# A graph layer on one core: the last edge column of every tenth tile, fetched by SyncE row by row

## The chip, the core and the metric

The kernel runs on one core of a Trainium2 chip. The metric is the device time of one execution in microseconds (us), the median of several runs. A core has five engines with an instruction list each: TensorE (PE in the profile, its weight loads PEld), VectorE (DVE), ScalarE (ACT), GpSimd (POOL) and SyncE (SP). They meet through semaphores. Data moves by DMA: an engine issues a transfer, the transfer runs on the core's 16 DMA engines, and its end raises a semaphore by 16.

## The reference: what is computed

One layer of an attention network over a graph with 12500 nodes of 64 features and 400000 edges. Every edge goes from a node src to a node dst and has 64 features of its own; the edges are sorted by dst.

```python
h_src = nfeats[src]
h_dst = nfeats[dst]
z_att = concatenate([h_src, h_dst, efeats], axis=-1)
e = leaky_relu(z_att @ W_attn + b_attn, negative_slope=0.01)[:, 0]
m = concatenate([h_src, efeats], axis=-1) @ W_ne
emax = segment_max(e, dst, num_segments=N)
ex = exp(e - emax[dst])
denom = segment_sum(ex, dst, num_segments=N)
alpha = ex / denom[dst]
z = segment_sum(alpha[:, None] * m, dst, num_segments=N)
out = relu(concatenate([nfeats, z], axis=-1) @ W_out)
# and then: layernorm(x + out)
```

For each edge one row of x is needed, that of its source node. That is the gather `nfeats[src]`.

## The kernel before

**Tiles.** The edges are cut into 391 tiles of 1024 edges (the last has 640). A tile lies on 128 partitions with J = 8 edges each, so it has eight columns. A ring V of ten slots (RING) holds for each tile the gathered source rows (Vx, eight columns of 64 numbers and a one) and the edge's own features (Ve). Ten tiles are a turn; there are 39 turns and one last tile.

**GpSimd** (L370 to L394) fills Vx: for each tile it waits for the tile's source indices (idx_in) and for a free slot (v_free), and then issues eight indirect transfers at L372, each of which brings 128 rows of x to the 128 partitions. In the loop that starts at L381 these are 80 a turn. Their ends raise h_in of the slot.

**SyncE** (L248 to L353) issues all other loads. Its list for the step of a tile t (function `step`, L306) is: wait until VectorE has the edge scores of tile t - 7 (u_done), store them to memory (L265); load the dst numbers of that tile to all partitions (L260); wait for the store and spread the scores to all partitions (L270); load the source indices of tile t + 3 (L254); wait until slot t is free (v_free) and load the edge features of tile t (L257). SyncE takes its list strictly in order, so a wait holds up all that follows.

**VectorE**, for each tile n (`supertile`, L684): L658 weighs the edges of the window before, L697 to L712 find the bounds of the new window from the spread scores (L705 waits for u_in), L663 to L674 add the sums of earlier windows. Then it makes the scores of tile n + 2: it waits for that tile's edge features and gathered rows (L722 to L725), multiplies them by the attention weights (L594), sums (L599) and raises u_done.

**ScalarE** makes the exponentials and copies of turned weights, **TensorE** turns the weights (L837) and multiplies them with the rows in V (L844), and tells when a slot is free. At the head of a turn VectorE, ScalarE and TensorE each load a list of counts from SBUF into registers (`counts`).

Of the kernel before, what the change touches and what calls it, by code (L numbers as in the profile page):

```python
# [27 lines left out]
P = 128  # L28
# [17 lines left out]
KEEP = 1e30  # L46
TINY = 1e-30
CB = 14


def graph_attention(nc, x, src, dst, ef, w_ne, w_att, b_att, w_out, out):
# [10 lines left out]
    NR = NB - 8 * OCT  # L62
    assert TURNS * RING == NT - 1 and JL * P + (NT - 1) * ST == E and 4 < JL < J
    assert 0 < NR <= 4 and OCT >= 4 and OCT % 2 == 0 and E >= ST
    assert YT * YS == PAIRS and 2 * PAIRS == NB and YS <= RING and YT < TURNS - 1
    chunks = [(b, min(CB, NB - b)) for b in range(0, NB, CB)]

    ctx = ExitStack()
    with ctx:
        def sb(name, shape, dt=F32):  # L70
            return ctx.enter_context(nc.sbuf_tensor(name, shape, dt))
# [36 lines left out]
        Vx = Vs[:, :, 0:J * XW].rearrange("p s (j w) -> p s j w", w=XW)  # L108
        Ve = Vs[:, :, EF_AT:EF_AT + J * F].rearrange("p s (j f) -> p s j f", f=F)
        srcs = sb("srcs", [P, RING, J], U32)  # L110
        dbc = sb("dbc", [P, 2, ST], I32)
        ubc = sb("ubc", [P, 2, ST])
        dnone = sb("dnone", [P, ST - JL * P], I32)
# [53 lines left out]
        idx_in = [sem(f"idx_in{s}") for s in range(RING)]  # L167
        ef_in = [sem(f"ef_in{s}") for s in range(RING)]
        h_in = [sem(f"h_in{s}") for s in range(RING)]
        bounds_out = sem("bounds_out")  # L170
        trip_in = sem("trip_in")
        lowf_in = sem("lowf_in")
# [56 lines left out]
        def freed(s, k):  # L229

            return k + (1 if s == RING - 1 else 0)

        def width(o):

            return 8 if not isinstance(o, int) or 0 <= o < OCT else NR if o == OCT else 0
# [12 lines left out]
        @block.sync  # L248
        def _(sp):

            full = NT - 1

            def load_src(t, s):
                sp.dma_start(srcs[:, s, :], edge_rows(src, t).rearrange("(p j) -> p j", j=J).bitcast(U32)).then_inc(idx_in[s], 16)  # L254

            def load_ef(t, s):
                sp.dma_start(Ve[:, s, :, :], (ef[bass.ds(t * ST, ST), :]).rearrange("(p j) f -> p j f", j=J)).then_inc(ef_in[s], 16)  # L257

            def load_dst(t, r):
                sp.dma_start(dbc[:, r, :], edge_rows(dst, t).rearrange("(a e) -> a e", a=1).broadcast_to((P, ST))).then_inc(d_in[r], 16)  # L260

            def store_scores(n, r):

                sp.wait_ge(u_done, n + 1)
                sp.dma_start(scores[r, :].rearrange("(p j) -> p j", j=J), u[:, r, :]).then_inc(u_out, 16)  # L265

            def spread_scores(n, r):

                sp.wait_ge(u_out, 16 * n + 16)
                sp.dma_start(ubc[:, r, :], scores[r:r + 1, :].broadcast_to((P, ST))).then_inc(u_in[r], 16)  # L270

            for s in range(2):
                load_src(s, s)
            sp.dma_start(wa[:, :], w_att.rearrange("a b -> b a").broadcast_to((P, 3 * F))).then_inc(w_in, 16)
            sp.dma_start(ba[:, :], b_att.rearrange("(a b) -> a b", a=1).broadcast_to((P, 1))).then_inc(w_in, 16)
            sp.dma_start(wne[:, :], w_ne[:, :]).then_inc(w_in, 16)
            sp.dma_start(wo_z[:, :], w_out[F:2 * F, :]).then_inc(w_in, 16)
            for s in range(2, RING):
                load_src(s, s)
            sp.wait_ge(wo_cleared, 1)  # L280
            for i in range(2):
                sp.dma_start(wo_xx[i * F:(i + 1) * F, i * F:(i + 1) * F], w_out[0:F, :]).then_inc(w_in, 16)

            for s in range(3):
                load_ef(s, s)
            for r in range(2):
                load_dst(r, r)

            sp.wait_ge(bounds_ready, 2)
            sp.dma_start(bounds_i.rearrange("(c p) k -> p c k", p=P), bi[:, :, :]).then_inc(bounds_out, 16)  # L290
            sp.dma_start(bounds_f.rearrange("(c p) k -> p c k", p=P), bf[:, :, :]).then_inc(bounds_out, 16)
            for s in range(3, 6):
                load_ef(s, s)
            sp.wait_ge(bounds_out, 32)
            sp.dma_start(trip[:, :], bounds_i.rearrange("t k -> (t k)").rearrange("(a b) -> a b", a=1)).then_inc(trip_in, 16)
            sp.dma_start(lowf[:, :, :], bounds_f[0:NT, :].rearrange("t k -> (t k)").rearrange("(a b) -> a b", a=1).broadcast_to((P, NT * 2)).rearrange("p (t k) -> p t k", k=2)).then_inc(lowf_in, 16)
            for n in range(2):
                store_scores(n, n)
                spread_scores(n, n)
            for s in range(6, RING):  # L300
                load_ef(s, s)
            for n in range(2, LEAD):
                store_scores(n, n % 2)
                load_dst(n, n % 2)
                spread_scores(n, n % 2)
            def step(k, s):  # L306

                t, n, r = RING * k + s, RING * k + (s - RING + LEAD), (s + LEAD) % 2
                store_scores(n, r)
                load_dst(n, r)  # L310
                spread_scores(n, r)
                if not isinstance(k, int) or s + AHEAD < RING:
                    ahead = (s + AHEAD) % RING
                    sp.wait_ge(h_in[ahead], 16 * J * (k + (1 if s + AHEAD >= RING else 0)))
                    load_src(t + AHEAD, ahead)
                sp.wait_ge(v_free[s], freed(s, k))
                load_ef(t, s)

            for s in range(AHEAD):
                sp.wait_ge(h_in[s], 16 * J)  # L320
                load_src(RING + s, s)
            with sp.Fori(1, TURNS - 1) as k:
                for s in range(RING):
                    step(k, s)
            for s in range(RING):
                if s == RING - AHEAD:
                    sp.wait_ge(h_in[0], 16 * J * TURNS)
                    sp.dma_start(srcs[:, 0, 0:JL], src[full * ST:E].rearrange("(p j) -> p j", j=JL).bitcast(U32)).then_inc(idx_in[0], 16)
                step(TURNS - 1, s)

            for s in range(RING - LEAD):
                n = full - RING + LEAD + s
                store_scores(n, n % 2)
                load_dst(n, n % 2)
                spread_scores(n, n % 2)
                if s == 0:
                    sp.wait_ge(v_free[0], TURNS)
                    sp.dma_start(Ve[:, 0, 0:JL, :], ef[full * ST:E, :].rearrange("(p j) f -> p j f", j=JL)).then_inc(ef_in[0], 16)
            sp.wait_ge(u_done, full + 1)
            sp.dma_start(scores[full % 2, 0:JL * P].rearrange("(p j) -> p j", j=JL), u[:, full % 2, 0:JL]).then_inc(u_out, 16)  # L340
            sp.wait_ge(dnone_set, 1)
            sp.dma_start(dbc[:, full % 2, 0:JL * P], dst[full * ST:E].rearrange("(a e) -> a e", a=1).broadcast_to((P, JL * P))).then_inc(d_in[full % 2], 16)
            sp.dma_start(dbc[:, full % 2, JL * P:ST], dnone[:, :]).then_inc(d_in[full % 2], 16)
            spread_scores(full, full % 2)

            for o in range(OCT):
                sp.wait_ge(rows_ready, o + 1)
                sp.dma_start(out[o * 8 * P:(o + 1) * 8 * P, :].rearrange("(b p) f -> p b f", p=P), y0[:, 8 * o:8 * o + 8, :]).then_inc(out_done, 16)
            sp.wait_ge(rows_ready, OCT + 1)
            n = NR - 1  # L350
            outs = OCT + 1
            if n:
                sp.dma_start(out[8 * OCT * P:(NB - 1) * P, :].rearrange("(b p) f -> p b f", p=P), y0[:, 8 * OCT:NB - 1, :]).then_inc(out_done, 16)  # L353
                outs += 1
            sp.dma_start(out[(NB - 1) * P:N, :], y0[0:NL, NB - 1, :]).then_inc(out_done, 16)
            sp.wait_ge(out_done, 16 * outs)

        @block.gpsimd
        def _(pool):
# [14 lines left out]

            for s in range(RING):
                pool.wait_ge(idx_in[s], 16)
                gather(s, J)
            if TURNS > 1:
                arrived = pool.alloc_register("arrived")
                behind = pool.alloc_register("behind")  # L380
                with pool.Fori(1, TURNS) as k:  # L381
# [4 lines left out]
                    for s in range(RING):  # L386
                        pool.wait_ge(pool_step, 2)
                        pool.wait_ge(idx_in[s], indices)

                        pool.wait_ge(v_free[s], k if s < RING - 1 else passed)  # L390
                        gather(s, J)
            pool.wait_ge(idx_in[0], 16 * TURNS + 16)
            pool.wait_ge(v_free[0], TURNS)
            gather(0, JL)  # L394
# [138 lines left out]
        def _(dve):  # L533
# [150 lines left out]
            def supertile(k, s, left, y_steps=None):  # L684
# [35 lines left out]
                if left >= 2:  # L720
                    done = t + 3 if isinstance(t, int) else produced
                    dve.wait_ge(ef_in[s2], 16 * k2 + 16)  # L722
                    if not isinstance(t, int):
                        dve.reg_mov(produced, t + 3)
                    dve.wait_ge(h_in[s2], 16 * J * k2 + 16 * (J if left != 2 else JL))  # L725
                    if y_steps is not None:
                        dve.wait_ge(y_ready, y_steps + 1)
                    edge_product(s2).then_inc(prod_done, 1)
# [210 lines left out]
```

## Time and profile before

| | |
|---|---|
| time, median of 3 runs | 4009.97 us (4007.27 to 4010.44) |
| the profiled execution: time | 4021.12 us |
| its span in the trace | 4019.2 us |
| busy in the span: GpSimd, VectorE | 2972.2 us (74%), 2837.8 us (71%) |
| busy in the span: TensorE, ScalarE | 2260.2 us (56%), 2020.9 us (50%) |
| indirect transfers issued by GpSimd | 3125 |
| mean granted TensorE clock | 0.592 |

The profile comes from one execution; its span runs from the first to the last instruction and is 2 us shorter than the execution's own time. Transfers that an engine only issues are not counted as its busy time: SyncE has no busy time at all there, and its work is seen in the timeline (rows with SPq) and in its waits. GpSimd's gathers are counted.

### The profile page before, as it was taken

How to read it: one execution, taken by the hardware profiler on the slowest of the kernel's cores; microseconds unless marked ns; L12 is line 12 of the kernel's file. 1: busy time of each engine (PE TensorE's matmuls, PEld its weight loads, DVE VectorE, ACT ScalarE, POOL GpSimd, SP SyncE). 2: the span in 40 equal slices, each digit the busy share in tenths (PEclk: the TensorE clock that was granted, in tenths of full speed). 3: DMA queues.
4: the chain of work that ended last, by engine and by line, in shares of the span. 5: the costliest groups of instructions: out<-in, count | busy, mean ns of one | idle time of the engine just before them, and what ended most of it. 6: DMA issues, size and time to landing. Idle time of an engine off the chain costs nothing.

```text
span 4019.2 us, 47762 instructions
## 1 busy us (share of the span) xinstructions
PE 2260.2 (56%) x9822; PEld 2005.2 (50%) x9823; DVE 2837.8 (71%) x5649; ACT 2020.9 (50%) x3433; POOL 2972.2 (74%) x3133
## 2 busy tenths in 40 slices
PE   2666655555555555555555555555555555555556
PEld 1555555544454444454444444544444544454456
DVE  8776666666766767676676766676767676766777
ACT  2665555544454444444444444444444444444446
POOL 7777777777777777777777777777777777777770
PEclk9665556556556565555655555555655556555557
DMA  6655555555555555555555555555555555555542
GB/s 166 177 173 156 159 157 156 160 158 157 158 157 157 157 157 157 157 157 157 158 157 157 157 157 157 157 158 157 157 157 157 157 157 158 157 157 157 158 147 66
DMA packets 409354, 627.14 MB, mean 156 GB/s; under 512 B 208412, under 2 KB 208796, under 8 KB 409332
## 3 DMA queue, kind: packets, MB, share of 16 engines
q1 hardware_dynamic: 296260, 519.51, 40.7%
q0 software_dynamic: 100000, 102.60, 12.3%
q10 hardware_dynamic: 13072, 4.80, 0.6%
q14 instruction: 16, 0.13, 0.0%
q8 instruction: 6, 0.10, 0.0%
HBM read 621.58 MB, written 4.81 MB: 156 GB/s over the span
## 4 chain that ended last, share of the span: by engine, by line
POOL 73%; issue 24%; DVE 1%; PE 1%; POOLq 1%; ACT 0%; DMA 0%; DVEq 0%
POOL V L372 73%; POOLq L390 0%; PE psE L909 0%; POOLq L381 0%; PE psT L902 0%; PE psG L844 0%; DVE y L801 0%; DVE var L782 0%; DMA V<-in_x_dram,srcs 0%; DVE y L778 0%; DVE mean L791 0%; DVE y L798 0%; DVE prod L785 0%; DMA srcs<-in_src_dram 0%; ACT zb L522 0%
## 5 line engine op out<-in xcount | busy, mean ns | idle before, releaser
L372 POOL DMA_INDIRECT V<-in_x_dram,srcs x3125 | 2971.2, 951 | 956.0 <-issue 952.9
L844 PE MATMUL psG<-V,pT 128*128 128x130 f32 x6250 | 1461.4, 427 | 366.6 <-DVE psS L663 366.6
L844 PEld LDWEIGHTS psG<-V,pT 128*128 128x128 f32 x6250 | 1361.5, 330 | 506.1 <-DVE psS L663 506.1
L837 PE MATMUL psT<-ident,e 128*128 128x128 f32 x3125 | 720.8, 404 | 1286.3 <-DVE e L658 1286.3
L448 ACT COPY pT<-psT 128x512 f32<-128x512 f32 x784 | 420.9, 589 | 1714.8 <-PE psT L837 1708.9
L837 PEld LDWEIGHTS psT<-ident,e 128*128 128x128 f32 x3125 | 573.8, 215 | 1392.7 <-DVE e L658 1392.7
L594 DVE TENSOR_TENSOR prod<-V,psM 128x512 f32<-128x512 f32 x782 | 502.4, 684 | 637.6 <-DMA V<-in_x_dram,srcs 621.8
L658 DVE TENSOR_TENSOR e<-zb,psE 128x1024 f32<-128x1024 f32 x392 | 478.8, 1221 | 259.4 <-DVE u L599 162.1
L705 DVE CUSTOM_DVE_ANT_0 um<-ubc,psS 128x1024 f32<-128x1024 f32 x391 | 477.6, 1221 | 20.2 <-ACT psS L461 19.3
L599 DVE TENSOR_REDUCE u<-prod 128x8 f32<-128x1024 f32 x391 | 477.0, 1220 | 13.5
L469 ACT ACTIVATE psE<-um,ebias 128x1024 f32<-128x1024 f32 x391 | 437.2, 1118 | 12.8
L461 ACT ACTIVATE psS<-dbc,nbias 128x1024 f32<-128x1024 int32 x391 | 437.1, 1118 | 12.7
L470 ACT ACTIVATE zb<-um,ebias 128x1024 f32<-128x1024 f32 x391 | 443.2, 1133 | 0.0
L669 DVE TENSOR_TENSOR acc<-acc,psS 128x260 f32 x393 | 167.4, 426 | 59.0 <-DVE psS L663 21.9
L674 DVE TENSOR_TENSOR acc<-acc,alpha 128x260 f32 x392 | 168.9, 431 | 56.2
L663 DVE TENSOR_TENSOR psS<-psG,half 128x260 f32<-128x260 f32 x393 | 171.4, 436 | 3.0 <-PE psT L888 1.8
L712 DVE SCALAR_TENSOR_TENSOR node<-keep,nn,node (+1 forms) x391 | 87.8, 225 | 69.0 <-DVE nn L710 67.4
L459 ACT ACTIVATE nbias<-nidbias,wshift 128x1 f32 x391 | 110.6, 283 | 46.5 <-issue 45.9
L467 ACT ACTIVATE ebias<-wnode,nn 128x3 f32<-128x3 f32 x391 | 120.5, 308 | 6.4 <-DVE nn L710 6.1
L473 ACT ACTIVATE alpha<-half,ebias 128x2 f32 x391 | 109.7, 281 | 0.0
L708 DVE SCALAR_TENSOR_TENSOR bounds<-slopes,cmax,wnode 128x3 f32<-128x3 f32 x391 | 87.5, 224 | 14.0
L700 DVE TENSOR_TENSOR wnode<-picked 128x3 f32<-128x3 f32 x391 | 64.7, 165 | 13.6
(97 smaller groups left out, 524.7 us busy)
## 6 DMA issues: line engine op xcount, KB each, us to landing
ubc<-scores SPq DMA_DIRECT2D x391, 512.0 KB
dbc<-in_dst_dram SPq DMA_DIRECT2D x390, 512.0 KB, 4.0
V<-in_edge_attr_dram SPq DMA_DIRECT2D x390, 256.0 KB, 2.8
V<-in_x_dram,srcs POOLq DMA_INDIRECT x3125
srcs<-in_src_dram SPq DMA_DIRECT2D x390, 4.0 KB
scores<-u SPq DMA_DIRECT2D x390, 4.0 KB
out_dram<-y SPq DMA_DIRECT2D x12, 256.0 KB
xt<-in_x_dram ACTq DMA_DIRECT2D x6, 448.0 KB, 14.2
```

The costliest lines, as they stand in the source:

```text
L372: nc.gpsimd.indirect_dma_start(Vx[:, s, j, 1:XW], None, x[:, :], bass.IndirectOffsetOnAxis(ap=srcs[:, s, j:j + 1], axis=0)).then_inc(h_in[ ...
L448: nc.scalar.copy(pT[:, i, :], psT[:, i, :]).then_inc(pt[i], 1)
L461: nc.scalar.activation(psS[:, :], dbc[:, s % 2, :], ACT.Square, bias=nbias[:, 0:1], scale=FAR).then_inc(sq_done, 1)
L469: nc.scalar.activation(psE[:, :], um[:, :], ACT.Exp, bias=ebias[:, 1:2], scale=SLOPE)
L470: nc.scalar.activation(zb[:, :], um[:, :], ACT.Exp, bias=ebias[:, 0:1]).then_inc(e_done, 1)
L594: last = nc.vector.tensor_tensor(prod[:, k * J * F:(k + 1) * J * F].rearrange("p (j f) -> p j f", f=F), rows, wa_v[:, k:k + 1, :].broadcas ...
L599: return nc.vector.tensor_reduce(u[:, i, :], prod[:, :].rearrange("p (k j f) -> p j k f", k=2, f=F), AXY, ALU.add)
L658: nc.vector.tensor_tensor(e1[:, :], zb[:, :], psE[:, :], ALU.max).then_inc(mx_done, 1)
L663: nc.vector.tensor_tensor(shares, psG[:, 0:AW].unsqueeze(1).broadcast_to((P, 2, AW)), half[:, bass.ds(tb, 1), :].rearrange("p a k -> p (a ...
L705: nc.vector.tensor_tensor_reduce(out=um[:, :], in0=ubc[:, r, :], in1=psS[:, :], scale=1.0, scalar=-3e38, op0=ALU.subtract, op1=ALU.max, ac ...
L837: last = nc.tensor.transpose(psT[:, i, (j - 4 * i) * P:(j - 4 * i + 1) * P], e1[:, 0:n * P].rearrange("q (p j) -> q j p", j=n)[:, j, :], i ...
L844: last = nc.tensor.matmul(psG[:, 0:AW], pT[:, i, (j - 4 * i) * P:(j - 4 * i + 1) * P], V[:, LEADIN + s * SLOT + XW * j:LEADIN + s * SLOT + ...
```

## The change

Slot 9 of the ring (OWN) is gathered differently. GpSimd issues only seven of its eight columns (`gathers`), so it issues 79 gathers a turn. The eighth column's 128 rows are fetched by SyncE. It first loads the 128 source indices of that column into one partition (`rowi`). In `load_rows` it loads 19 of them into registers, and issues for each a transfer of one row of x, with the register as offset, to one partition of Vx. The 128 rows are spread over seven steps of SyncE's loop: 19 rows in the step of slot 9 itself, behind its load of edge features, then 19 in each of the steps of slots 0 to 4 and 14 in that of slot 5, each between the load of source indices and the wait for the free slot. VectorE waits for the four semaphores of these rows before the edge product of such a tile.

```diff
+OWN = RING - 1
+BUNCH = 19
+BUNCHES = -(-P // BUNCH)
...
+        rowi = sb("rowi", [1, P], I32)
...
+        rowi_in = sem("rowi_in")
+        row_in = [sem(f"row_in{q}") for q in range(4)]
...
+        def gathers(s):
+
+            return J - 1 if s == OWN else J
...
+            row = [sp.alloc_register(f"row{i}") for i in range(BUNCH)]
+
+            def load_row_indices(t):
+
+                sp.dma_start(rowi[:, :], edge_rows(src, t).rearrange("(p j) -> j p", j=J)[J - 1:J, :], allow_slow_non_contiguous=True).then_inc(rowi_in, 16)
+
+            def load_rows(k, c):
+
+                first, last = c * BUNCH, min(P, (c + 1) * BUNCH)
+                sp.load(row[0:last - first], rowi[0:1, first:last])
+                for i in range(last - first):
+                    p = first + i
+                    at = sp.snap(row[i], min_val=0, max_val=N - 1)
+                    sp.dma_start(Vx[p:p + 1, OWN, J - 1, 1:XW], x[bass.ds(at, 1), :]).then_inc(row_in[p // 32], 16)
...
+            load_row_indices(OWN)
...
-                    sp.wait_ge(h_in[ahead], 16 * J * (k + (1 if s + AHEAD >= RING else 0)))
+                    sp.wait_ge(h_in[ahead], 16 * gathers(ahead) * (k + (1 if s + AHEAD >= RING else 0)))
                     load_src(t + AHEAD, ahead)
+                if s < BUNCHES - 1:
+                    load_rows(k - 1, s + 1)
                 sp.wait_ge(v_free[s], freed(s, k))
+                if s == OWN:
+                    sp.wait_ge(rowi_in, 16 * k + 16)
                 load_ef(t, s)
-
+                if s == OWN - 1:
+                    load_row_indices(t + 1)
+                if s == OWN:
+                    load_rows(k, 0)
+
+            sp.wait_ge(rowi_in, 16)
+            load_rows(0, 0)
...
-                gather(s, J)
+                gather(s, gathers(s))
...
-                        gather(s, J)
+                        gather(s, gathers(s))
...
-                    dve.wait_ge(h_in[s2], 16 * J * k2 + 16 * (J if left != 2 else JL))
+                    dve.wait_ge(h_in[s2], 16 * gathers(s2) * k2 + 16 * (gathers(s2) if left != 2 else JL))
+                    if s2 == OWN:
+                        for q in range(4):
+                            dve.wait_ge(row_in[q], 512 * k2 + 512)
```

How this stands in the built programs, first on SyncE, in the loop, the step of slot 0 before. A row is line, operation, tile written and read, with the semaphore it waits for; ISA here is a fused register instruction.

```order
L265 DMA scores<-u 128x8 [waits u_done]
L260 ISA
L260 DMA dbc<-in_dst_dram 128x1024
L269 ISA
L270 DMA ubc<-scores 128x1024 [waits u_out]
L314 REGISTER_ALU
L254 ISA [waits h_in3]
L254 DMA srcs<-in_src_dram 128x8
L257 ISA [waits v_free0]
L257 DMA V<-in_edge_attr_dram 128x512
```

The same step of the changed kernel, up to its second row. The last two rows of it come 19 times in the step before the wait for v_free0.

```order
L276 DMA scores<-u 128x8 [waits u_done]
L271 ISA
L271 DMA dbc<-in_dst_dram 128x1024
L280 ISA
L281 DMA ubc<-scores 128x1024 [waits u_out]
L341 REGISTER_ALU
L265 ISA [waits h_in3]
L265 DMA srcs<-in_src_dram 128x8
L292 TENSOR_LOAD rowi
L295 ISA
L296 DMA V<-in_x_dram 1x64
```

Between the load of source indices and the edge features there is now a register load and 19 pairs of a register instruction and a row transfer; nothing that stood in the step has changed its place against its neighbours.

On VectorE, in the changed kernel, the edge product of a tile in slot 9 (prod is the product, u the scores):

```order
L763 ISA [waits ef_in9]
L767 ISA [waits h_in9]
L633 TENSOR_TENSOR prod<-V,psM 128x512 [waits row_in2,row_in3,row_in1,row_in0]
L633 TENSOR_TENSOR prod<-V,psM 128x512
L638 TENSOR_REDUCE u<-prod 128x8 [waits prod_done]
```

The first product now waits for the rows; the scores behind it, for which SyncE waits at the head of a step, wait with it.

## Rows read from the trace of the kernel before

**Rows 1.** The page: DMA in all; the chain that ended last, by engine.

```profile
DMA packets 409354, 627.14 MB, mean 156 GB/s; under 512 B 208412, under 2 KB 208796, under 8 KB 409332
...
POOL 73%; issue 24%; DVE 1%; PE 1%; POOLq 1%; ACT 0%; DMA 0%; DVEq 0%
```

**Rows 2.** The page's groups: line, engine, operation | busy us, mean ns | idle before, releaser.

```profile
L372 POOL DMA_INDIRECT V<-in_x_dram,srcs x3125 | 2971.2, 951 | 956.0 <-issue 952.9
```

**Rows 3.** Timeline of VectorE, first tile of a turn: start us, us, line, operation.

```profile
2041.91 1.22 DVE L658 TENSOR_TENSOR e<-zb,psE 128x1024 f32<-128x1024 f32 x1 [2.42 <-issue]
...
2047.25 1.28 DVE L594 TENSOR_TENSOR prod<-V,psM 128x512 f32<-128x512 f32 x2 [0.27 <-issue]
2048.57 1.22 DVE L599 TENSOR_REDUCE u<-prod 128x8 f32<-128x1024 f32 x1
2050.24 1.22 DVE L658 TENSOR_TENSOR e<-zb,psE 128x1024 f32<-128x1024 f32 x1 [0.45 <-DVE u L599]
```

**Rows 4.** Waits: engine, line <- waited for: us in total, times, longest.

```profile
DVE prod L594 <- DMA V<-in_x_dram,srcs: 621.8, 333, 3.1
...
DVE e L658 <- DVE u L599: 162.1, 351, 0.5
...
DVE e L658 <- issue: 94.9, 39, 3.2
...
ACT nbias L459 <- issue: 45.9, 32, 2.1
```

**Rows 5.** Waits of SyncE's issues.

```profile
SPq L265 <- DVE u L599: 1620.5, 390, 17.8
SPq L257 <- PEq L869: 1077.0, 376, 5.0
SPq L270 <- DMA scores<-u: 235.8, 384, 2.8
```

**Rows 6.** Timeline of SyncE, one step and the next step's start.

```profile
2010.34 0.33 SPq L265 DMA_DIRECT2D scores<-u  x1
2010.86 0.33 SPq L260 DMA_DIRECT2D dbc<-in_dst_dram  x1
2011.76 0.33 SPq L270 DMA_DIRECT2D ubc<-scores  x1
2012.29 0.33 SPq L254 DMA_DIRECT2D srcs<-in_src_dram  x1
2015.59 0.33 SPq L257 DMA_DIRECT2D V<-in_edge_attr_dram  x1
2019.33 0.33 SPq L265 DMA_DIRECT2D scores<-u  x1
```

**Rows 7.** Timeline of SyncE at the start: eight index transfers; trip and the next.

```profile
3.85 6.04 SPq L254 DMA_DIRECT2D srcs<-in_src_dram  x8
...
31.75 0.30 SPq L295 DMA_DIRECT2D trip<-bounds_i  x1
32.09 0.34 SPq L296 DMA_DIRECT2D lowf<-bounds_f  x1
```

**Rows 8.** The page's DMA issues: count, KB each, us to landing.

```profile
V<-in_edge_attr_dram SPq DMA_DIRECT2D x390, 256.0 KB, 2.8
```

More of the change, by code:

```diff
@@ L64, in graph_attention @@
     assert 0 < NR <= 4 and OCT >= 4 and OCT % 2 == 0 and E >= ST
+    assert BUNCHES <= RING - LEAD
     assert YT * YS == PAIRS and 2 * PAIRS == NB and YS <= RING and YT < TURNS - 1
@@ L338, in _ @@
                     sp.dma_start(Ve[:, 0, 0:JL, :], ef[full * ST:E, :].rearrange("(p j) f -> p j f", j=JL)).then_inc(ef_in[0], 16)
+                if s < BUNCHES - 1:
+                    load_rows(TURNS - 1, s + 1)
             sp.wait_ge(u_done, full + 1)
```

## The prediction

> **What bounds the kernel now.** I read the chain of waits first: 73% of it is one line, GpSimd's gather, and 24% is issue time in front of it [rows 1]. The group of that line has 3125 gathers with 2971.2 us busy and 956.0 us of idle time before them, which the engine spent issuing [rows 2]. So one gather costs (2971.2 + 956.0) / 3125 = 1.257 us, and GpSimd waits for nobody. A turn of the ring is ten tiles of eight gathers: 80 x 1.257 = 100.5 us. With 391 tiles that is the span, less the start and the last part.
>
> Next I asked who stands right behind. VectorE waits 621.8 us in 333 waits for gathered rows before its edge product [rows 4], so it keeps up. Its own time for one tile is read where it did not wait: from the L658 that starts at 2041.91 to the next at 2050.24 is 8.33 us [rows 3]. At the head of each turn it loads twenty counts into registers; the idle time there is 94.9 us over 39 turns, 2.43 us each, against 162.1 / 351 = 0.46 us on the other tiles [rows 4]. The load of twenty costs 1.97 us.
>
> Then SyncE, which the page does not count as an engine and which the change loads. Its waits are 1620.5 us for the scores (u_done), 1077.0 us for a free ring slot and 235.8 us for the scores' way to memory [rows 5]. The first two are its room: 2697.5 / 390 = 6.9 us a step, 69 us a turn. Its work in a step is in the timeline [rows 6]: scores at 2010.34, dst at 2010.86, the spread at 2011.76 (behind the scores' round trip), src at 2012.29, and the edge attributes at 2015.59, when the slot came free.
>
> **What goes.** Slot 9 is gathered with seven columns, not eight. It is filled by 39 tiles (9, 19, ... 389), so GpSimd loses 39 x 1.257 = 49 us, and its turn becomes 79 x 1.257 = 99.3 us. That is all that can be won.
>
> **What comes, on SyncE.** Per turn there are 128 one-row transfers, each behind one fused register instruction, seven loads of 19 (the last 14) indices into registers, and one transfer of 128 indices. No row of before shows a one-row transfer with a register offset on SyncE, so it is bounded.
> - Below: the transfer onto one partition, trip, is 0.30 us, and the next starts 0.34 us after it [rows 7]. With the register instruction free, 0.34 us a row.
> - Above: eight index transfers back to back took 6.04 us at the start, 0.76 us each [rows 7].
> - Nearest: in the loop src follows the spread with one register instruction and an offset in a register, as a row will: 2012.29 - 2011.76 = 0.53 us, 0.33 of it the transfer, so 0.2 for the rest [rows 6]. With trip's 0.30 in place of 0.33 that is 0.50 us. I take 0.50.
>
> The loads of 19 registers are near VectorE's 1.97 us for twenty; ScalarE's loads of ten leave 45.9 / 32 = 1.43 us of idle time [rows 4]. Both gaps hold the jump back to the loop's head as well; ten registers more cost 1.97 - 1.43 = 0.54 us, so by the slope alone 19 would be 1.03 us. I take 1.9 us and keep 1.03 and 1.97 as ends.
>
> The Trainium skill gives `tensor_load` a floor of about 600 ns ("DMA: Bandwidth & Descriptors", Latency and other measured facts). Both gaps in this trace are more than twice that; with the floor as the price the turn worked out below would be, as an estimate, 7 x 1.3 = 9 us shorter and the time 355 us less.
>
> Alone, 128 x 0.50 + 7 x 1.9 = 77 us a turn against 69 us of room. But the room is not where the rows are: seven of the ten steps carry them all, and SyncE takes its list in order. Behind the rows in a step stand the edge attributes, and behind these the next tile's scores and their spread, without which VectorE can't go on with that tile. So a step that is longer than a gathered tile (10.05 us) delays VectorE, and the light steps can't give it back, since their scores exist only after VectorE has done another tile. The turn, from SyncE's own list:
> - Steps 0 to 4, full: 1.95 from the scores to src [rows 6], 0.52 for src, 1.9 load, 19 x 0.50 = 9.5, and 0.52 for the edge attributes, whose slot is long free by then: 14.4 us, five times 72.0.
> - Step 5, the last 14 rows: 1.95 + 0.52 + 1.9 + 7.0 = 11.4 us. These rows are the last of the tile whose edge product comes next on VectorE. So this product waits for them: 1.4 us to land (what scores takes from its issue to the spread, 2010.34 to 2011.76 [rows 6]), then product and sum, 2.5 us (prod at 2047.25 to 2049.79 [rows 3]), until the next scores exist: 15.3 us.
> - Steps 6 to 8, light, at VectorE's pace: 3 x 8.33 + 1.97 for its counts = 27.0 us.
> - Step 9: its rows stand behind the edge attributes, which leave 5.25 us after the scores (2010.34 to 2015.59 [rows 6]): 5.25 + 0.52 + 1.9 + 9.5 = 17.2 us.
>
> The sum is 131.5 us a turn. GpSimd's 99.3 us vanish under it. Against 100.5 us that is 31.0 us more, 39 times: 1209 us. The profiled execution took 4021 us, so it becomes 5230; the median of the runs is 11 us lower, 5219. I forecast 5220 us.
>
> **What the rest costs.** The 128 indices of a turn are fetched a step ahead in a light step: nothing, and if that cover fails, one round trip of about 1.4 us a turn, 55 us in all. VectorE's four new waits stand before the edge product; queued behind them are the score sum, its u_done and the next tile, on which ScalarE and TensorE hang. That is the wait already in step 5. The src and edge loads run some seven tiles ahead; they come later but not late. The 4992 rows carry 1.3 MB beside 627 MB [rows 1]. What I leave out is that in full steps the edge attributes (2.8 us to landing [rows 8]) leave just before the next scores; the longest wait for a scores' round trip is 2.8 us [rows 5] against a mean of 0.6, so a full step may grow by up to 2.2 us, 11 us a turn. That is in the upper end.
>
> Each 0.01 us of the row is 1.28 us a turn and 50 us of the time. With 0.34 a row and loads of 1.03 us: 52.4 + 12.2 + 27.0 + 13.3 = 104.9 us a turn, 4180 us. With 0.62 a row, or 0.53 and the longer round trips: about 147 us, some 5820 us.
>
> **The rivals.**
> 1. Faster: SyncE's room swallows the rows. The turn above is 67.5 + 128 times the row's cost, so GpSimd still sets the pace if a row costs under (99.3 - 67.5) / 128 = 0.25 us, or under 0.30 us with loads of 1.03 us. Then it is 4010 - 49 = 3961 us. For it: trip was not followed by a stall, and a row is narrower than any transfer shown. Against: no transfer of SyncE in this trace takes under 0.30 us. Chance 0.08; and 0.02 that it ends within 0.2% of before.
> 2. The waits overlap better than I say, and only SyncE's sum counts. Its work without the rows is 1.95 + 0.53 + 0.52 = 3.0 us a step, 30 us a turn; with 77 us, 107 us, 39 x 6.5 = 254 us more: about 4265. For it: the scores are stored two tiles ahead. Against: two tiles of lead are 17 us, and the full steps overrun by 7 x 4. Chance 0.10.
> 3. The register load costs its slope alone, 1.03 us, and the rest of the gaps that I read belongs to the jump at the loop's head, which SyncE's bunches don't make: 7 x 0.87 = 6 us less, a turn of 125.4 us, 971 us more, 4980. For it: both gaps shown stand at a loop's head. Against: ScalarE's load of ten would then be under half of its gap. Chance 0.10. The Trainium skill's floor, above, leans the same way.
> 4. The rows back up in SyncE's transfer queue, as the eight index transfers did: 0.76 us a row, 33 us more a turn than forecast, 6500 us. Against: those stood behind wide transfers at the start. Chance 0.08.
>
> **How the numbers follow.** The forecast keeps 0.62, its own range 4700 to 5750 (0.40 to 0.60 us a row). The range of 8 in 10 runs from the lower bound of the turn to the longer round trips: 4180 to 5820; left out are rival 1 with its even case, 0.10, rival 4, 0.08, and a little of the tail. Within 0.2%, 8 us, no change can be told from none. Faster 0.08, same 0.02, slower 0.90.
>
> **What would show it.** Right: GpSimd's gathers wait for free slots, and the chain of waits runs through SyncE; row transfers start 0.47 to 0.55 us apart; a gap of about 1.9 us stands before each bunch; steps of 14 us, seven in ten; VectorE waits for spread scores in full steps, and for the rows once a turn. Wrong: rows 0.30 us apart or closer, or an untouched GpSimd chain at 99.3 us a turn. If the rows are 0.50 us apart and the turn is still near 107 us, the overlap was misjudged and not the price.

## The result, and the profile after

The changed kernel takes 5603.19 us (5600.80 to 5606.78), the kernel before 4008.70 us: 1.3975 times the time, with a 95% interval of 1.3957 to 1.3993. The forecast was 5220 us, with 4180 to 5820 as range. So it is slower by the mechanism that was forecast, and with a loss a third larger than forecast (1594 us for 1210).

The page of the changed kernel: the instruction transfers, the chain that ended last by engine and by line, and the group of the gathers.

```profile
q14 instruction: 240, 1.97, 0.1%
...
SPq 47%; issue 19%; DVE 17%; DMA 12%; DVEq 3%; PE 1%; ACT 1%; ACTq 1%; PEld 0%; PEldq 0%
SPq L296 22%; SPq L292 16%; DMA scores<-u 10%; SPq L295 4%; DVE prod L633 4%; DVE u L638 3%; DVE um L744 3%; SPq L268 2%; SPq L265 2%; SPq L281 1%; DVE psS L702 1%; DVEq L777 1%; DVE acc L708 1%; DMA V<-in_x_dram 1%; DVE e L697 1%
...
L411 POOL DMA_INDIRECT V<-in_x_dram,srcs x3086 | 2927.2, 949 | 2509.8 <-PEq L911 1653.6
```

The chain has left GpSimd [rows 1] and runs through SyncE's own list. The gathers still take 0.95 us each, but in front of them stand 2509.8 us of idle time where there were 956.0 [rows 2], and most of it now waits for TensorE to free a slot. GpSimd's 39 gathers fewer are worth nothing.

SyncE's waits, in the same form as [rows 5]:

```profile
SPq L276 <- DVE u L638: 428.4, 160, 17.3
SPq L281 <- DMA scores<-u: 404.0, 389, 3.6
SPq L268 <- PEq L911: 383.1, 114, 5.0
```

The wait for the scores fell from 1620.5 to 428.4 us and that for a slot from 1077.0 to 383.1 (a further 103.1 us of it stand at another line, for slot 9): SyncE is now late where it was early. Only the wait for the scores' round trip grew, from 235.8 to 404.0 us. Who waits for SyncE is seen in the waits of the others:

```profile
POOL V L411 <- PEq L911: 1653.6, 288, 19.8
...
DVE um L744 <- DMA ubc<-scores: 1044.3, 140, 9.2
...
DVE prod L633 <- DMA V<-in_x_dram: 738.4, 39, 20.9
```

GpSimd waits for free slots, VectorE for the spread scores, and once a turn (39 times) for the last rows, 738.4 / 39 = 18.9 us each. In 69 further waits, 411.1 us, VectorE's line L744 waits for ScalarE, which waits in its turn for the dst numbers (2049.9 us) that SyncE loads just behind the scores. The timeline of SyncE shows why: the step of slot 9 from its edge features on, the whole step of slot 0, the spread in that of slot 1, and the row part of slot 3's (start us, us, line, operation).

```profile
2750.98 0.33 SPq L268 DMA_DIRECT2D V<-in_edge_attr_dram  x1
2753.34 8.20 SPq L296 DMA_DIRECT2D V<-in_x_dram  x19
2764.23 0.37 SPq L276 DMA_DIRECT2D scores<-u  x1
...
2766.04 0.33 SPq L281 DMA_DIRECT2D ubc<-scores  x1
2766.66 0.33 SPq L265 DMA_DIRECT2D srcs<-in_src_dram  x1
2771.30 7.86 SPq L296 DMA_DIRECT2D V<-in_x_dram  x19
2779.36 0.36 SPq L268 DMA_DIRECT2D V<-in_edge_attr_dram  x1
2779.84 0.36 SPq L276 DMA_DIRECT2D scores<-u  x1
...
2782.03 0.33 SPq L281 DMA_DIRECT2D ubc<-scores  x1
...
2815.51 0.33 SPq L265 DMA_DIRECT2D srcs<-in_src_dram  x1
2817.91 8.09 SPq L296 DMA_DIRECT2D V<-in_x_dram  x19
```

The step of slot 0 takes 2779.84 - 2764.23 = 15.6 us, where a gathered tile takes 10.05. Its 19 rows take 2779.36 - 2771.30 = 8.06 us, 0.42 us each. Between src and the first row lie 4.64 us in this step, but 2.40 us in that of slot 3. The chain of waits has the register loads (L292) as pieces of their own:

```profile
2706.29 3.06 SPq L292
...
2715.06 1.17 DMA V<-in_x_dram
...
2761.72 2.41 issue
...
2767.03 4.09 SPq L292
...
2815.90 1.80 SPq L292
```

A load of the same 19 registers takes 4.09 us in one step and 1.80 us in another; the load of 14 takes 3.06. The last row lands 1.17 us after its issue. And at the loop's jump there are 2.41 us of issue time in which SyncE does nothing. Last, the row transfer itself (line, operation, count: shortest, median and longest in ns); a register move of 29 ns stands at the same line before each:

```profile
L296 SPq DMA_DIRECT2D V<-in_x_dram x4992: 224/228/308, 73.0 to 5508.5; - x200
```

### The profile page after: what moved, and what is told of

The parts are those of the page before. It is cut to its first block, busy times and chain, and to the rows that moved or that the text cites. A ratio compares the mean times of both kernels' runs of the same rounds, so it can differ in the third digit from the quotient of the medians.

```text
span 5599.3 us, 63276 instructions
## 1 busy us (share of the span) xinstructions
PE 2165.4 (39%) x9822; PEld 1936.0 (35%) x9823; DVE 2840.6 (51%) x5649; ACT 2047.7 (37%) x3433; POOL 2928.1 (52%) x3094
## 3 DMA queue, kind: packets, MB, share of 16 engines
q14 instruction: 240, 1.97, 0.1%
## 4 chain that ended last, share of the span: by engine, by line
SPq 47%; issue 19%; DVE 17%; DMA 12%; DVEq 3%; PE 1%; ACT 1%; ACTq 1%; PEld 0%; PEldq 0%
SPq L296 22%; SPq L292 16%; DMA scores<-u 10%; SPq L295 4%; DVE prod L633 4%; DVE u L638 3%; DVE um L744 3%; SPq L268 2%; SPq L265 2%; SPq L281 1%; DVE psS L702 1%; DVEq L777 1%; DVE acc L708 1%; DMA V<-in_x_dram 1%; DVE e L697 1%
## 5 line engine op out<-in xcount | busy, mean ns | idle before, releaser
L411 POOL DMA_INDIRECT V<-in_x_dram,srcs x3086 | 2927.2, 949 | 2509.8 <-PEq L911 1653.6
L744 DVE CUSTOM_DVE_ANT_0 um<-ubc,psS 128x1024 f32<-128x1024 f32 x391 | 477.6, 1221 | 1455.7 <-DMA ubc<-scores 1044.3
L879 PE MATMUL psT<-ident,e 128*128 128x128 f32 x3125 | 630.8, 365 | 1450.4 <-DVE e L697 1450.4
L879 PEld LDWEIGHTS psT<-ident,e 128*128 128x128 f32 x3125 | 508.8, 208 | 1556.8 <-DVE e L697 1556.8
L633 DVE TENSOR_TENSOR prod<-V,psM 128x512 f32<-128x512 f32 x782 | 502.5, 684 | 779.0 <-DMA V<-in_x_dram 738.4
L498 ACT ACTIVATE nbias<-nidbias,wshift 128x1 f32 x391 | 113.6, 290 | 2106.2 <-DMA dbc<-in_dst_dram 2049.9
```

Source lines behind the costliest of these rows:

```text
L411: nc.gpsimd.indirect_dma_start(Vx[:, s, j, 1:XW], None, x[:, :], bass.IndirectOffsetOnAxis(ap=srcs[:, s, j:j + 1], axis=0)).then_inc(h_in[ ...
L633: last = nc.vector.tensor_tensor(prod[:, k * J * F:(k + 1) * J * F].rearrange("p (j f) -> p j f", f=F), rows, wa_v[:, k:k + 1, :].broadcas ...
L744: nc.vector.tensor_tensor_reduce(out=um[:, :], in0=ubc[:, r, :], in1=psS[:, :], scale=1.0, scalar=-3e38, op0=ALU.subtract, op1=ALU.max, ac ...
L879: last = nc.tensor.transpose(psT[:, i, (j - 4 * i) * P:(j - 4 * i + 1) * P], e1[:, 0:n * P].rearrange("q (p j) -> q j p", j=n)[:, j, :], i ...
```

## The experiments

The kernel before took 4009.74 us on the chip of the runs shift, bunch20, rows_fixed and loads_only, and 4009.10 us on that of the others. Line numbers move a little between kernels.

**Why a register load takes 1.8 or 4.1 us.** The two fast loads begin at element 0 and 76 of the index row, which are multiples of 16 bytes; the slow ones begin at 19, 38, 57, 95 and 114. The first experiment moves the index row by one element.

```diff
-        rowi = sb("rowi", [1, P], I32)
+        rowi = sb("rowi", [1, P + 4], I32)
...
-                sp.load(row[0:last - first], rowi[0:1, first:last])
+                sp.load(row[0:last - first], rowi[0:1, first + 1:last + 1])
```

> The changed kernel with the index row moved by one element (4 bytes) in its partition, everything else the same. Theory A, address: the bunches that begin at a multiple of 16 bytes are now the second and the sixth (bytes 80 and 384), so the loads in the steps of slots 0 and 4 take 1.80 us and those of slots 9 and 3 take 4.07; the time stays within 50 us of 5600, as two of seven are fast either way. Rival B, place: the loads in the steps of slots 9 and 3 stay at 1.80 us.

One run: 5612.19 us. SyncE's timeline of that kernel, in slot 9's step (edge features, then rows), slot 0's and slot 4's (src, then rows):

```profile
2617.75 0.33 SPq L268 DMA_DIRECT2D V<-in_edge_attr_dram  x1
2622.37 8.20 SPq L296 DMA_DIRECT2D V<-in_x_dram  x19
...
2635.80 0.33 SPq L265 DMA_DIRECT2D srcs<-in_src_dram  x1
2638.18 7.85 SPq L296 DMA_DIRECT2D V<-in_x_dram  x19
...
2698.92 0.33 SPq L265 DMA_DIRECT2D srcs<-in_src_dram  x1
2701.28 7.85 SPq L296 DMA_DIRECT2D V<-in_x_dram  x19
```

The step of slot 9 now has 4.62 us before its rows, where it had 2.36, and those of slots 0 and 4 have 2.38 and 2.36, where they had 4.64. Nothing but the address had moved: the address it is, and not the place in the list. The second experiment makes every bunch begin at a multiple of 16 bytes.

```diff
-BUNCH = 19
+BUNCH = 20
```

> The changed kernel with bunches of 20 rows (the last has 8) in place of 19 (the last 14). In the changed kernel's trace a load of 19 indices takes 1.80 us in two of seven bunches and 4.07 us in four, the load of 14 takes 3.06. Theory A, address: the fast ones begin at byte 0 and 304 of the index row, multiples of 16, the slow ones do not; with 20 every bunch begins at a multiple of 80 bytes, so all loads of 20 take about 1.85 us and that of 8 under 1.2. Per turn: four loads save 2.2 us each, the last 2 us, its six rows fewer 2.5 us in the step that VectorE waits for, the others 0.5 us more each: about 11 us less, 420 us over 39 turns, near 5180 us. Rival B, place: the slow loads are slow where they stand in SyncE's list (instruction supply); then the same steps stay slow and the time is within 50 us of 5600.

5064.38 us (5054.88 to 5066.21), 1.2622 of the kernel before (1.2601 to 1.2643). Its loads, of 20 and (shortest) 8 registers, and those of two kernels shown further down, all of 16 and all of 12 (shortest, median and longest in ns):

```profile
L292 SPq TENSOR_LOAD <-rowi x273: 712/1394/1427, 71.8 to 4961.6; - x137
...
L293 SPq TENSOR_LOAD <-rowi x273: 1137/1171/1201, 72.1 to 4463.4; - x137
...
L293 SPq TENSOR_LOAD <-rowi x273: 934/945/975, 71.8 to 3941.2; - x137
```

A load of 20 takes 1.40 us, less than the aligned load of 19 with its 1.80. That odd remainder was not foreseen, and it is why the time came out 116 us under the expected 5180. The rows give its price: from 8 to 12, 16 and 20 registers an aligned load grows by 0.22 to 0.23 us for each four; the aligned 19 stands 0.63 us above 16, 0.21 us for each of three single ones; and from 14 to 19 an unaligned load grows by 1.01 us, 0.20 us a register. As an estimate from these rows, a load that begins at a multiple of 16 bytes pays for each full four registers about what it pays for one left over, and a load that does not begin there pays that for every register. So 539 of the 1594 us were a matter of where the index bunches begin and how many they hold.

**What a row costs, and whether the list is the bound.** The next kernel issues as many transfers, 128 a turn, from fixed rows of x (not the rows that the edges need), without register loads and register instructions.

```diff
-                sp.load(row[0:last - first], rowi[0:1, first:last])
...
-                    at = sp.snap(row[i], min_val=0, max_val=N - 1)
-                    sp.dma_start(Vx[p:p + 1, OWN, J - 1, 1:XW], x[bass.ds(at, 1), :]).then_inc(row_in[p // 32], 16)
+                    sp.dma_start(Vx[p:p + 1, OWN, J - 1, 1:XW], x[p:p + 1, :]).then_inc(row_in[p // 32], 16)
```

> The changed kernel with its 128 row transfers a turn, but each from a fixed row of x, so without the register loads and without the register instruction (the last column of each tenth tile gets the wrong rows). Theory: SyncE's own list is the bound, and a row's 0.42 us is 0.23 us of transfer and 0.19 us of register instruction. Rows then stand about 0.27 us apart, a full step is 3.0 us, some 1 us longer round trip and 5.1 us of rows, which is less than the 9.93 us of a gathered tile, and GpSimd sets the pace again with 99.3 us a turn: 3960 to 4030 us. Rival: rows stand 0.42 us apart whatever stands between them, since the transfer queue takes no more; then only the loads go, 23 us a turn of 140, about 117 us a turn, near 4710 us.

4001.14 us (3998.33 to 4004.09), 0.9977 of the kernel before (0.9967 to 0.9987). From SyncE's timeline of it, the rows of slot 9's step and the step behind the loop's jump:

```profile
2662.36 5.62 SPq L294 DMA_DIRECT2D V<-in_x_dram  x19
2668.46 0.35 SPq L276 DMA_DIRECT2D scores<-u  x1
...
2671.12 5.63 SPq L294 DMA_DIRECT2D V<-in_x_dram  x19
2676.95 0.36 SPq L268 DMA_DIRECT2D V<-in_edge_attr_dram  x1
```

19 rows take 2676.95 - 2671.12 = 5.83 us, 0.31 us each: of the 0.42 us, 0.11 goes with the register work (the fused instruction and the move) and 0.31 stays with the transfer, not 0.27. A full step, from scores to scores, is 9.0 us here and 9.7 to 10.2 us in the next four, about a tile's share of a turn with 79 gathers (9.93). The page says the same:

```profile
q14 instruction: 18, 0.15, 0.0%
...
SPq 39%; DVE 22%; DMA 17%; issue 15%; DVEq 4%; PE 2%; ACT 1%; ACTq 1%; PEld 0%; PEldq 0%
...
L409 POOL DMA_INDIRECT V<-in_x_dram,srcs x3086 | 2932.3, 950 | 943.9 <-issue 915.1
```

The gathers are back at 943.9 us of idle time, but the chain still runs through SyncE. At 0.31 us a row and with no loads the two engines are level, and of the 49 us that the 39 gathers are worth 9 arrive. Behind the last row of slot 9's step the next scores follow 0.48 us later, over the same jump; in the changed kernel they follow after 2.69 us (2753.34 + 8.20 to 2764.23). Its instruction transfers are 18, about as many as before (16), where the changed kernel has 240, some six more a turn: it seems that the longer loop fetches its instructions again each turn, which was not tested by itself.

The next edit was to leave the other half alone, the loads without rows, with all 80 columns gathered:

```diff
-            return J - 1 if s == OWN else J
+            return J
...
-                for i in range(last - first):
-                    p = first + i
-                    at = sp.snap(row[i], min_val=0, max_val=N - 1)
-                    sp.dma_start(Vx[p:p + 1, OWN, J - 1, 1:XW], x[bass.ds(at, 1), :]).then_inc(row_in[p // 32], 16)
```

> The changed kernel with the index transfer and the seven register loads a turn, but without the 128 row transfers; GpSimd gathers all 80 columns again. Theory: a full step is then 3.0 us and a load of up to 4.07 us, 7.1 us, under the 10.05 us of a gathered tile, and all of it is hidden: within 20 us of 4009. Rival: SyncE's extra time shows whatever the room, 23 us a turn: near 4900 us.

One run: 4010.22 us, as expected, but not for the reason expected: the trace of this run holds none of the 273 register loads. Source indices and edge features of the step of slot 2:

```profile
2077.05 0.33 SPq L265 DMA_DIRECT2D srcs<-in_src_dram  x1
2079.63 0.33 SPq L268 DMA_DIRECT2D V<-in_edge_attr_dram  x1
```

They are 2.58 us apart, where the load between them takes 4.07 us in the changed kernel. No instruction of this kernel reads the registers any more, and the built program does not load them. So the run shows only that the index transfer of each turn costs nothing. What the loads cost without the rows is not shown by any run.

**The round trip of the scores.** In the kernel with bunches of 20 the edge features are loaded before the rows:

```diff
-                if s < BUNCHES - 1:
-                    load_rows(k - 1, s + 1)
                 sp.wait_ge(v_free[s], freed(s, k))
...
                 load_ef(t, s)
+                if s < BUNCHES - 1:
+                    load_rows(k - 1, s + 1)
```

> Bunches of 20, and in each step the edge features are loaded before the rows, no longer behind them and just before the next scores. In the kernel with bunches of 20 the spread leaves 1.75 us after the scores in the first full step and 1.76 to 2.67 us after them in the others, against 0.9 to 1.5 us in light steps. Theory: the scores' short store queues behind the 256 KB of edge features issued half a microsecond before it; with the rows in between, the round trip in full steps falls back to about 1.5 us, 0.7 us less in six steps, up to 5 us a turn: 4860 to 4960 us. Rival: the rows themselves hold the scores back; then the round trip stays near 2.1 us and the time within 40 us of 5064.

4931.90 us (4925.26 to 4937.04), 1.2299 of the kernel before (1.2278 to 1.2319). The scores and their spread in a full step of it, and then in one of the kernel with bunches of 20:

```profile
2629.72 0.36 SPq L276 DMA_DIRECT2D scores<-u  x1
...
2631.17 0.33 SPq L281 DMA_DIRECT2D ubc<-scores  x1
```

```profile
2643.44 0.36 SPq L276 DMA_DIRECT2D scores<-u  x1
...
2646.11 0.33 SPq L281 DMA_DIRECT2D ubc<-scores  x1
```

From the scores to the spread 1.45 us, against 2.67. Over the whole runs SyncE's wait for the scores' round trip falls from 385.7 to 213.1 us. The short store stood behind the 256 KB issued half a microsecond before it; with the rows between the two it does not. The changed kernel itself shows the same: in its step of slot 0, where the rows of slot 9 stand between the two, the spread follows the scores after 1.8 us (2764.23 to 2766.04), in the step of slot 1 after 2.2 us (2779.84 to 2782.03). The new order is worth 132 us.

**VectorE's wait for the rows, and where the step begins to show.** Here SyncE's list is kept, with bunches of 20, but the rows land in a spare tile; GpSimd gathers all 80 columns, and VectorE waits for no row. Two more kernels do so with 16 and 12 rows in each of the seven steps.

```diff
-            return J - 1 if s == OWN else J
+            return J
...
-                    sp.dma_start(Vx[p:p + 1, OWN, J - 1, 1:XW], x[bass.ds(at, 1), :]).then_inc(row_in[p // 32], 16)
+                    sp.dma_start(spare[p:p + 1, :], x[bass.ds(at, 1), :]).then_inc(row_in[p // 32], 16)
...
-                    if s2 == OWN:
-                        for q in range(4):
-                            dve.wait_ge(row_in[q], 512 * k2 + 512)
```

> SyncE's list as with bunches of 20, but the rows land in a spare tile that nobody reads; GpSimd gathers all 80 columns and VectorE waits for no row. Theory: most of the loss is SyncE's list between the scores of successive tiles; VectorE's wait for the last rows adds what it costs to rebuild its lead, about 7 us of the 126.7 us a turn: near 4790 us (4700 to 4880). Rival, the wait for the rows is the loss: then the time falls to within 100 us of 4010. Rival, that wait costs nothing since SyncE is late anyway: within 40 us of 5064.

One run: 4839.99 us, 224 us under the kernel with bunches of 20 that uses the rows. VectorE's wait for them is a fifth of the loss with bunches of 20 (224 of 1055 us); the rest is the list itself.

> As the run with unused rows, but 16 rows in each of seven steps (112 a turn). Theory: a full step is 1.95 + 0.7 + 0.52 + 1.2 + 16 x 0.418 + 0.52 = 11.6 us, longer than a gathered tile of 10.05; six of them, the step of slot 9 and three light ones make about 110 us a turn: near 4400 us (4280 to 4480). Rival, only SyncE's sum counts: 30 + 112 x 0.418 + 7 x 1.2 = 85 us a turn, under 100.5, so 4010 us.

One run: 4562.19 us, 82 us above the expected range.

> As the run with unused rows, but 12 rows in each of seven steps (84 a turn). Theory: a full step is 1.95 + 0.7 + 0.52 + 1.0 + 12 x 0.418 + 0.52 = 9.7 us, just under a gathered tile's 10.05, so it is all but hidden: 4010 to 4080 us. If rows cost whatever the room, 84/128 of the loss of the run with all rows unused would show, some 500 us.

One run: 4032.74 us. The scores of a full step and of the next one with 16 rows; then the same with 12, with the spread between, and the scores at both ends of the step of slot 6 and of that of slot 9:

```profile
2609.80 0.36 SPq L277 DMA_DIRECT2D scores<-u  x1
...
2622.39 0.36 SPq L277 DMA_DIRECT2D scores<-u  x1
```

```profile
2614.89 0.36 SPq L277 DMA_DIRECT2D scores<-u  x1
...
2617.54 0.33 SPq L282 DMA_DIRECT2D ubc<-scores  x1
...
2625.20 0.37 SPq L277 DMA_DIRECT2D scores<-u  x1
...
2666.71 0.42 SPq L277 DMA_DIRECT2D scores<-u  x1
...
2670.73 0.33 SPq L277 DMA_DIRECT2D scores<-u  x1
...
2691.70 0.33 SPq L277 DMA_DIRECT2D scores<-u  x1
...
2706.39 0.37 SPq L277 DMA_DIRECT2D scores<-u  x1
```

A full step takes 12.6 us with 16 rows and 10.3 us with 12, 1.0 and 0.6 us above the sum in the expectations; 0.5 of that is the round trip, which was 2.65 us (2614.89 to 2617.54) and not the 2.1 that they held. With 12 the step is a little over the gathered tile of 10.05 and 24 us show; with 16 it is 2.5 us over and 553 us show.

One long step by itself does not show. With 12 rows the step of slot 9 takes 14.7 us, and yet only 24 us are lost in the run: the step of slot 6 takes 4.0 us, so SyncE catches up there. What shows is a row of steps that are each longer than a gathered tile.

No version here that fetches the right rows is faster than the kernel before. VectorE's wait for the rows comes on top of the list, and even 12 rows a step (84 a turn) without that wait were not quite hidden, where 128 would be needed.

## Why the prediction was right, and where its sizes were off

**The bound moved to SyncE's list, in order: right.** The chain, the gathers' wait for slots, and VectorE's waits for spread scores and once a turn for the rows are those that were named. Rival 1 (the room swallows the rows) needed 0.25 to 0.30 us a row; the kernel with fixed rows at 0.31 us and no loads only just gets there. Rival 2 (only SyncE's sum counts) is out: with 16 unused rows a step the time is 4562 us where the sum of its work is under a gathered turn: 85 us in the expectations, 96 us with the longer round trips ((586 - 236) / 39 = 9.0 us a turn) and the jump. That the excess of the full steps over 10.05 us decides, and not the sum, is shown by the runs with 12 and 16 rows. That the light steps can't give anything back holds for the changed kernel, where they ran at VectorE's pace, but not in general: with 12 unused rows the step of slot 6 took 4.0 us. Of the signs, the spacing of the rows missed (0.42 us, where 0.47 to 0.55 was named), as did the gap of 1.9 us in five of seven bunches and the steps of 14 us (15.6 us in slot 0, 18.6 in slot 9).

**The step-by-step turn: close, with errors both ways.** From the step that starts at 2702.81 to that at 2843.18 a turn takes 140.4 us, forecast 131.5.

| part of a turn, us | forecast | measured |
|---|---|---|
| steps 0 to 4 | 72.0 | 79.0 |
| step 5, until the next scores | 15.3 | 16.1 |
| steps 6 to 8, VectorE's pace | 27.0 | 26.7 |
| step 9 | 17.2 | 18.6 |
| in these: 128 rows | 64.0 | 53.8 (0.42 each) |
| in these: seven loads | 13.3 | 22.9 (2 x 1.80 + 4 x 4.07 + 3.06) |
| in these: scores to spread, steps 0 to 5 | 8.5 | 14.2 |
| in these: the loop's jump | 0 | 2.4 |

The mis-sized terms are the register load first. It was taken as 1.9 us from the idle time of VectorE and ScalarE at a turn's head. But the trace of before has these loads as rows of their own, VectorE's and then ScalarE's (shortest, median and longest in ns):

```profile
L735 DVEq TENSOR_LOAD <-trip x39: 1357/1365/1615, 60.0 to 3846.9; - x39
...
L478 ACTq TENSOR_LOAD <-trip x39: 2127/2141/2332, 59.6 to 3843.8; - x39
```

VectorE's load of twenty neighbouring counts takes 1.37 us, not 1.97, and ScalarE's load of ten, every second one of the same list, 2.14 us, not 1.43: idle time was no price of a load, and the slope read from it had the wrong sign. That 1.9 came near the 1.80 us of an aligned load of 19 is luck. Five of seven loads were not aligned, and the forecast did not ask where a bunch begins. That is 9.6 us a turn, 374 us of the time. Rival 3 leaned to the wrong side. The Trainium skill's floor of 600 ns ("DMA: Bandwidth & Descriptors", Latency and other measured facts) is not a floor here: at the end of the kernel before, ScalarE loads a single count in 0.30 us and VectorE two in 0.55. As a price it was off by up to seven times (4.07 us).

The round trip of the scores is the second: 5.7 us a turn. It had been named as left out and put into the upper end; the run with the edge features first showed its cause. The jump of SyncE's own loop, 2.4 us, was put at nothing, without a reason.

The row was too dear by 0.08 us: 10.2 us a turn the other way. The nearest row carried a transfer of 0.33 us and a rest of 0.2; a one-row transfer is busy 0.228 us, with a register move of 0.03 before it, and 19 of them showed no back-up in the queue (rival 4). So it is partly luck that the forecast of 131.5 came out as near as it did: the cheaper rows hid 10.2 of the 17.7 us by which loads, round trips and jump were too cheap. 39 turns at 140.4 us in place of 100.5 add 1556 us to the 4010 of before, 5566 us in all. The turn shown is a little short: 33 turns, from the scores at 367.04 to those at 5015.36, take 140.9 us on average, which gives 5586 us. The 17 us left are open.

**The landing and the light steps: right.** The last row landed in 1.17 us (1.4 forecast), and the three light steps at VectorE's pace took 26.7 us.

## What to carry to other kernels

An engine that only issues transfers has room in each step, not in the sum: compare the steps of its list that carry the new work one behind the other with the pace of the bound, and count all that stands behind the new work in that list. One long step can be made up for, six in a row were not. Price a step by its parts on that engine (transfer, register instruction, register load) from the rows of these parts, not from idle time, and ask of each whether it depends on address and size. And when a test kernel leaves something out, look in its trace whether the rest is still there. And look at which long transfer is issued just before a short one that somebody waits for.

## What the runs showed of the hardware that was not expected

- A load of registers from SBUF on SyncE takes 0.71 us for 8 registers, 0.95 us for 12, 1.17 us for 16, 1.40 us for 20 and 1.80 us for 19 when it begins at a multiple of 16 bytes, and 4.07 us for 19 and 3.06 us for 14 when it does not. Moving the same list by 4 bytes moved the slow loads with it. A load of every second count is dear too: ten took 2.14 us on ScalarE.
- SyncE issues one-row transfers 0.31 us apart from fixed addresses and 0.42 us apart with a fused register instruction and a register move before each.
- In the changed kernel SyncE's next scores left 2.69 us after the last row, over the jump, with 240 instruction transfers in the run; with 12 rows a step 2.85 us after it (2698.24 + 5.30 to 2706.39), with 202; with the shorter loop of fixed rows 0.48 us after it, with 18. That the fetch of instructions is the cause is read from these counts and was not tested by itself.
- A 4 KB store issued half a microsecond after a 256 KB load on the same engine took 2.2 us (slot 1 of the changed kernel) to 2.67 us (bunches of 20) for its round trip in the steps shown; with ten or more between them it took 1.45 and 1.8 us.
